# Rope attention: the three-part split of the negated maxima moved from VectorE to GpSimd

## The reference, cut to what matters

```python
q = _apply_rope(q, sin, cos)            # 16 heads of 8, 1024 positions, 4 batches
k = _apply_rope(k, sin, cos)
attn = jnp.einsum('bhqd,bhkd->bhqk', q, k) / np.sqrt(DH)
attn = jax.nn.softmax(attn, axis=-1)    # needs each row's maximum
sa = jnp.einsum('bhqk,bhkd->bhqd', attn, v)
```

## Time and profile before

| | |
|---|---|
| median of the runs | 5364.67 us |
| the profiled execution's own time | 5366.84 us |
| its span, first to last instruction | 5365.2 us |
| busy TensorE / VectorE / ScalarE / GpSimd | 4808.4 / 3870.1 / 2519.6 / 797.4 us |
| stage 1 (loop) | about 175 to 940 us |
| stage 2 (loop) | about 1856 to 2592 us |
| instruction packets in the whole trace (queue q14) | 114, 0.93 MB, 8 KB each but for a few |

### The profile page before, as it was taken

One profiled execution on the slowest core, in us unless ns is written; L12 is line 12 of the kernel. 1 busy time (PEld: TensorE's weight loads), 2 busy tenths in 40 slices (PEclk: granted clock), 3 DMA queues, 4 the chain that ended last, 5 costly groups with the idle time before them and its releaser, 6 DMA issues. The chain is left out here.

```text
span 5365.2 us, 82244 instructions
## 1 busy us (share of the span) xinstructions
PE 4808.4 (90%) x22823; PEld 2214.2 (41%) x22823; DVE 3870.1 (72%) x8568; ACT 2519.6 (47%) x3338; POOL 797.4 (15%) x628
## 2 busy tenths in 40 slices
PE   3999999697997699999787999799999999997999
PEld 2222222444443222222443777344344344443776
DVE  6889899366666799999466777666666666666777
ACT  3466666313433377777422444344444444443444
POOL 3000000001002000000001000333333333332000
PEclk9899999798998799999898999899999999998999
DMA  3111111200000311111201000000000000001000
GB/s 92 35 42 36 41 41 37 80 0 29 0 0 9 79 42 42 42 40 39 92 0 35 1 0 0 11 8 8 8 8 5 7 8 8 8 8 38 1 0 16
DMA packets 195883, 133.33 MB, mean 25 GB/s; under 512 B 103852, under 2 KB 160600, under 8 KB 195736
## 3 DMA queue, kind: packets, MB, share of 16 engines
q1 hardware_dynamic: 187576, 114.00, 7.6%
q0 software_dynamic: 6432, 17.57, 1.4%
q10 hardware_dynamic: 1728, 0.28, 0.0%
HBM read 94.28 MB, written 36.44 MB: 24 GB/s over the span
## 5 line engine op out<-in xcount | busy, mean ns | idle before, releaser
L644 DVE TENSOR_REDUCE ra_mh<-PS 128x1 f32<-128x512 f32 x2144 | 1342.4, 682 | 177.9 <-PE PS L522 151.0
L599 ACT ACTIVATE ra_p<-PS 128x1024 f32<-128x1024 f32 x1040 | 1014.3, 1021 | 506.9 <-PE PS L529 501.5
L522 PE MATMUL PS<-ra_k,ra_q 96*128 96x512 bf16 x2144 | 757.1, 393 | 17.1 <-DVE ra_mh L644 16.9
L1835 POOL TENSOR_TENSOR ca_s<-ca_s,ca_p 128x1024 f32<-128x1024 f32 (+3 forms) x320 | 544.5, 1702 | 969.0 <-ACT ca_p L1792 969.0
L1792 ACT ACTIVATE ca_p<-PS 128x1024 f32<-128x1024 f32 (+3 forms) x384 | 311.4, 811 | 775.7 <-PE PS L1694 325.5
L538 PE MATMUL PS<-ra_p,ra_va 128*32 128x512 f32 x4192 | 574.8, 613 | 70.2 <-ACT ra_va L592 70.0
L529 PE MATMUL PS<-ra_q,ra_k 99*128 99x512 bf16 x2080 | 624.7, 381 | 1.7
L1694 PE MATMUL PS<-ca_q,ca_k 128*128 128x512 f32 (+3 forms) x1536 | 602.9, 506 | 5.0 <-DMA ca_q<-ca_nm 3.1
L522 PEld LDWEIGHTS PS<-ra_k,ra_q 96*128 96x128 bf16 x2144 | 202.1, 97 | 689.3 <-DVE ra_mh L644 530.2
L1440 ACT ACTIVATE f_hh<-PS,f_b 128x512 f32<-128x512 f32 x448 | 302.8, 687 | 389.7 <-PE PS L1396 389.4
L1406 PEld LDWEIGHTS PS<-f_w,f_hh 128*128 128x128 f32 x3584 | 432.9, 192 | 99.5 <-issue 66.0
(11 more groups left out here) (237 smaller groups left out, 5590.8 us busy)
## 6 DMA issues: line engine op xcount, KB each, us to landing
ra_k<-qk_parts SPq DMA_DIRECT2D x136, 144.0 KB
ra_q<-qk_parts SPq DMA_DIRECT2D x408, 48.0 KB
o_heads<-ra_ot POOLq DMA_DIRECT2D x134, 128.0 KB, 3.0
ao_ot<-o_heads SPq DMA_DIRECT2D x16, 1024.0 KB, 6.4
qk_parts<-rp_parts SPq DMA_DIRECT2D x96, 128.0 KB, 2.3
ca_w<-in_L_attn_W_qkv SPq DMA_DIRECT2D x34, 192.0 KB, 2.7
ra_vc<-v_heads SPq DMA_DIRECT2D x34, 128.0 KB, 5.2
v_heads<-rp_vs SPq DMA_DIRECT2D x64, 64.0 KB, 1.9
```

What stands on the lines that cost most here:

```text
L522: pe.matmul(PS[:, 5 + place % 3, :], Q[0:KMAX, u, j, t * P:(t + 1) * P], K[0:KMAX, u, j, h * BT:(h + 1) * BT], start=True, stop=True).then ...
L599: act.activation(PR[:, s % 2, PH * pair:PH * (pair + 1), :], PS[:, PH * pair:PH * (pair + 1), :], ACT.Exp, scale=float(DH) ** -0.5).then_i ...
L644: dve.tensor_reduce(mh[:, pair, c // HALVES, c % HALVES:c % HALVES + 1], PS[:, bank, :], AX.X, ALU.max).then_inc(s_max, 1)
L1835: pool.tensor_tensor(S[:, qc, :, off:BT], S[:, qc, :, off:BT], PR[:, s % 3, :, off:BT], ALU.add).then_inc(s_sum, 1)
```

## The change

GpSimd gets the four operations behind L633. `nm` is still written by VectorE, since it is read out of PSUM. The two roundings become additions of a zero tile. GpSimd's loop now has two groups in a pass and does the split between its stores. VectorE waits, ahead of L633, that the parts before have been made (`s_mp`), since it overwrites `nm`.

```diff
+        zero = sb("ra_zero", [PH * KT, P])
+        s_zero = sem("ra_zeroed")
...
-                with pool.Fori(0, ITERS) as n:
-                    for h in range(2):
-                        store(n, h)
+                def parts(number, passes, pair, u, rows):
+
+                    pool.wait_ge(s_max, number + 1)
+                    pool.wait_ge(s_mr[pair][u], rows)
+                    ch = Chain(pool, s_ch, 3 * passes)
+                    ch.link(pool.tensor_tensor(mp[:, pair, u, 0, :], nm[:, :], zero[:, :], ALU.add))
+                    ch.link(pool.tensor_tensor(nr[:, :], nm[:, :], mp[:, pair, u, 0, :], ALU.subtract))
+                    ch.link(pool.tensor_tensor(mp[:, pair, u, 1, :], nr[:, :], zero[:, :], ALU.add))
+                    pool.tensor_tensor(mp[:, pair, u, 2, :], nr[:, :], mp[:, pair, u, 1, :],
+                                       ALU.subtract).then_inc(s_mp, 1)
+
+                pool.memset(zero[:, :], 0.0).then_inc(s_zero, 1)
+                pool.wait_ge(s_zero, 1)
+                parts(PRO.index(("turn", 0)), 0, 0, 0, 0)
+                with pool.Fori(0, ITERS // 2) as it:
+                    for u in range(2):
+                        n = 2 * it + u
+                        store(n, 0)
+                        parts(len(PRO) + len(RING) * n + RING.index(("turn", 1)), 2 * n + 1, 1, u, 16 * PARTS * it)
+                        store(n, 1)
+                        parts(len(PRO) + len(RING) * n + RING.index(("turn", 0)), 2 * n + 2, 0, 1 - u,
+                              16 * PARTS * (it + u))
...
                     if use[0] == "turn":
-                        pair = use[1]
+                        dve.wait_ge(s_mp, passes)
                         dve.tensor_scalar(nm[:, :], PS[0:PH * KT, bank, 0:P], -1.0, None, ALU.mult).then_inc(s_max, 1)
-                        dve.wait_ge(s_max, number + 1)
-                        dve.wait_ge(s_mr[pair][u], rows)
-                        ch = Chain(dve, s_ch, 3 * passes)
-                        ch.link(dve.tensor_copy(mp[:, pair, u, 0, :], nm[:, :]))
-                        ch.link(dve.tensor_tensor(nr[:, :], nm[:, :], mp[:, pair, u, 0, :], ALU.subtract))
-                        ch.link(dve.tensor_copy(mp[:, pair, u, 1, :], nr[:, :]))
-                        dve.tensor_tensor(mp[:, pair, u, 2, :], nr[:, :], mp[:, pair, u, 1, :],
-                                          ALU.subtract).then_inc(s_mp, 1)
```

More of the change, by code:

```diff
@@ L625, in _, with read @@
             def _(dve):
-                def read(number, place, use, passes, u, rows):
+                def read(number, place, use, passes):
                     bank = 5 + place % 3
@@ L650, in _ @@
                 for i, use in enumerate(PRO):
-                    read(i, i, use, 0, 0, 0)
+                    read(i, i, use, 0)
                 with dve.Fori(0, ITERS // 2) as it:
@@ L655, in _ @@
                         for i, use in enumerate(RING):
-                            second = use == ("turn", 1)
-                            read(len(PRO) + len(RING) * n + i, len(PRO) + i, use, 2 * n + (1 if second else 2),
-                                 u if second else 1 - u, 16 * PARTS * (it if second else it + u))
+                            read(len(PRO) + len(RING) * n + i, len(PRO) + i, use, 2 * n + (1 if use == ("turn", 1) else 2))
 def broadcast_rows(ap, parts, n):
```

## The result

| | before | after |
|---|---|---|
| median of the runs | 5360.64 us (5 runs, 5354.17 to 5368.04) | 5387.13 us (5 runs, 5386.42 to 5388.43) |
| profiled execution, span | 5366.84 us, 5365.2 us | 5388.43 us, 5386.7 us |
| first to last turn, stage 1 | 737.4 us | 709.3 us |
| first to last turn, stage 2 | 710.5 us | 758.3 us |

The account below looks back on a forecast made before the run. TensorE was taken to set the pace, with VectorE close behind. From the profiled execution, 5366.84 - 2.6 - 2.1 - 26.9 + 47.9 = 5383.1 us, or 5381 us against the median; range 5356 to 5393 us.

Parts of the forecast that it names:

- The likeliest case: Stage 2's branch back stalls with a second wait: 5381 us, own range 5374 to 5391, chance 63%.
- step 5: VectorE's shorter stream moves both loops across instruction blocks: stage 1 loses its stalls, -26.9 us; stage 2 gains them, +47.9 us.
- step 1: Chain off VectorE inside the loops: 0.08 us at two of four turns a pass, -2.6 us.
- The second packet: Stage 2's branch back: VectorE waits for another instruction block, taken as 3.0 us a pass, between 2.3 and 3.84.
- The rival of no second wait: Stage 2's next block is still there or fetched with the first; stage 2 gives back 26.9 us: 5360 us, 17%.
- The faster rival: Stage 2's loop starts at 1088 or above, three blocks hold it, neither stage stalls: 5333 us, 18%.
- steps 1 and 2: Chain off VectorE: -2.6 us in the loops, and -2.1 us ahead of them, where nothing hides it.
- step 3: Chain on GpSimd at 0.46 us an operation: parts 1.1 us later, within the slack, cost 0.
- The rival of a late GpSimd: GpSimd's chain exceeds 4.5 us, so the pair's scores come late at 66 turns: +125 us, 5506 us, 2%.
- The slack of the first pair: At a turn, from the parts landing to the pair's first scores load: 3.3 us, in which 1.1 us later fits.
- step 4: GpSimd's operations beside VectorE's reads out of PSUM: costed at 0; 1.8 us a turn if each held up a read.

Follow-up runs that it names:

- the edge at 1471 and 1472: Kernel after with 111 memsets ahead of the second attention's prologue, stage 2's loop ending at 1471: 5339.61 us; with 112, ending at 1472: 5372.77 us.

## Why the prediction was right, point by point

The forecast was 5381 us with a stall in stage 2 of two packets' length; measured were 5387.13 us, 6 us more, with that stall. The likeliest case came in. As a change it was forecast at +16 us, against the median of 5364.67; it measured +26.5 us, 4 of them since the median of before came out lower with more runs.

**The blocks (step 5).** Stage 1: 737.4 - 709.3 = 28.1 us less, of which 1.3 is step 1's, so 26.8 for the 26.9 forecast. Stage 2: a kernel with the same loop and no stall takes 709.2 us, so the stall costs 49.1 us, or 7.01 a pass, where I put 6.84 and 47.9 us. The second packet, taken as 3.0 between 2.3 and 3.84, measured 7.01 - 3.84 = 3.2 us; this is the whole cost of a longer gap and of a longer stretch at a clock of 0.50 (5.5 us for 3.4, the last window of the earlier trace rows). The 3.84 us are (737.4 - 710.5) / 7, a stall of the kernel before. That they are more than its gap of 2.32 by the fall of the clock is borne out by the passes with 120 memsets, which cost 1.6 us more with the fall than without. The positions 154 to 427 and 1087 to 1360 and the start at 1088 are confirmed by what one memset and the edge at 1471 and 1472 did. The rival of no second wait rested on the next block's still being there; two packets inside one gap say that it is not.

**The faster rival**, no stall in either stage at 5333 us, is what one memset brings about (5338.11 us): it was right on the price, and in the kernel as changed one instruction was missing. The edges found here, at 1088 and 1472, are 384 = 3 x 128 apart, and two neighbouring packets, of 8 KB each, 126 and 129 instructions; the measurement decides for blocks of 128, for this chip and this engine. That four are kept is worked out from five packets a pass and from loops of three blocks that fetch nothing. Each loop here that touches four blocks stalls behind its branch back, at 2.57 to 7.13 us a pass, and none that touches three does.

**The chain on VectorE (steps 1 and 2).** In a loop it is worth 710.5 - 709.2 = 1.3 us a stage, 2.6 in all, as forecast; behind a `("turn", 0)` of the kernel after the next step takes 492.16 - 489.32 = 2.84 us, where it was 2.92. With the part ahead of the loops I had 4.7 us; the two kernels without stalls differ by 4.9.

**The chain on GpSimd (step 3).** Each operation takes 0.45 or 0.42 us (0.46 forecast). The parts leave 2.36 - 1.53 = 0.83 us later than before (1.1 forecast), and nobody waits. The slack of the first pair, 3.3 us for the kernel before and so 2.5 behind a chain that is 0.83 us later, measured some 2.7 us by the run with eight operations more. That this comes so close is luck in part, since the 1.7 us to landing were set behind the end of the last issue, 0.6 us too late. What I left out is that the slack is not the same at each turn: behind the change it is 3.9 us or more for the second pair, and no more than 1.4 us ahead of the loops. The rival of a late GpSimd, 5506 us, was far off in the kernel after. With eight operations more its wait comes, at 32 turns and not at 66.

**Both engines at once (step 4)** was costed at 0. VectorE's reads in the window 180 to 900 us, first before, then after, with min/median/max in ns:

```profile
L644 DVE TENSOR_REDUCE ra_mh<-PS x967: 667/681/693, 180.8 to 899.7; 128x1 f32<-128x512 f32 x194
```

```profile
L657 DVE TENSOR_REDUCE ra_mh<-PS x1007: 677/682/693, 179.8 to 899.1; 128x1 f32<-128x512 f32 x168
```

The median moved by 1 ns and the longest not at all. So nothing is seen of GpSimd holding up VectorE here, where VectorE's reads are out of PSUM; no run shows how VectorE would do beside these operations with its inputs in SBUF.

**What is left.** Against the profiled execution the sum was 5383.1 us, and it took 5388.43: 5.3 us more. 1.2 of them are the second packet's. Some 3.6 us lie between the two stages, from the last turn of the one to the first of the other (1845.6 - 899.8 = 945.8 us, where it was 942.2). It isn't the change: with 112 memsets this stretch took 943.2 us and with 111 945.8, in kernels that differ there by one memset. What makes it vary stays open.

## What to carry to other kernels

Before pricing an edit, ask whether it makes an engine's loop longer or shorter, or moves one that comes later in the stream: for a loop of some 270 to 300 instructions on VectorE, that was worth up to 49 us in a stage, ten times what the edit itself was worth (4.9 us). The signs are a gap without a cause at a loop's end, q14 packets in each pass, and one stage that is slower than its twin. To measure a change to such a kernel, compare the two versions with both loops laid so that they touch three blocks; the memsets that do this cost next to nothing where the engine is idle (5339.61 us with 111 of them, 5338.11 with two), and the best kernel here (5338.11 us, 0.9950 of before) is the change with one of them ahead of each attention.

## What I had not expected of the hardware

- The stall has several prices in one and the same kernel, by where the loop lies. In the kernel after it is 2.57 us a pass on average (loop start 9 instructions ahead of a block start, branch ninth in its block), 5.10 (branch first in its block) and 6.71 or 7.01 (loop start the last instruction of its block). In the kernel before it is 3.84 (34 instructions, branch twelfth), 5.13 (branch first) and 7.13 (loop start the last).
- The gap is longer where the branch stands first in its block, 3.52 and 3.77 us, than where it stands further in, 2.19 and 2.32. The packets suggest that the one asked for on entering the last block holds up the one that the branch needs.
- Gaps of VectorE of the same length, 2.18 to 2.27 us in one and the same loop, were followed by TensorE at a granted clock of 0.50 three times and at 1.00 four times; the fall cost 1.6 us each time.
